# Queries by seven products over pairs of heads, and the experts' stages behind half chunks, in a gated cross-attention layer

## What is computed

```python
def xattn(latents, context, Wq, Wk, Wv, Wo, q_norm_w, k_norm_w):
    kv = concatenate([context, latents], axis=1)              # 461 rows for each of 8 batches
    q = rms_norm(heads(latents @ Wq, 32), q_norm_w)
    k = rms_norm(heads(kv @ Wk, 8), k_norm_w)
    v = heads(kv @ Wv, 8)
    probs = softmax(einsum('bhgqd,bhkd->bhgqk', q, k) / sqrt(128))
    return merge(einsum('bhgqk,bhkd->bhgqd', probs, v)) @ Wo  # 4096 -> 1024
x = x + tanh(g_xattn) * xattn(layernorm(x), context, ...)
x = x + tanh(g_ffn) * experts(layernorm(x))                   # router, top 2 of 8, rank 16
```

## Time and profile before

| | us |
|---|---|
| three runs | 1750.63, 1753.11, 1757.34 |
| median | 1753.11 |
| profiled execution | 1748.85 |
| its span, first to last instruction | 1746.9 |
| granted TensorE clock, mean | 0.995 of full |
| projections end, first query matmul | 636.44 |
| slots 0 to 54 | about 684 to 1309 |
| last chunk ends | about 1701 |

### The profile page before, as it was taken

One profiled execution on the slowest core, in us unless ns is written; L12 is line 12 of the kernel. 1 busy time (PEld: TensorE's weight loads), 2 busy tenths in 40 slices (PEclk: granted clock), 3 DMA queues, 4 the chain that ended last, 5 costly groups with the idle time before them and its releaser, 6 DMA issues.

```text
span 1746.9 us, 26303 instructions
## 1 busy us (share of the span) xinstructions
PE 1692.9 (97%) x9312; PEld 1508.2 (86%) x9312; DVE 1170.6 (67%) x2074; ACT 879.1 (50%) x1655; POOL 730.5 (42%) x584
## 2 busy tenths in 40 slices
PE   7999999999999999999999999999998999999996
PEld 6788888678888879999999999999997888999994
DVE  6778876777777733777777777777766664455546
ACT  5455554454544423666666666666656654343321
POOL 1444543234443402666666666666665550000000
PEclk9999999999999999999999999999999999999999
DMA  5567778545566554344444333444444654665522
GB/s 193 163 185 237 231 213 247 140 145 173 158 176 161 138 214 144 120 122 123 131 130 123 119 122 120 131 131 130 127 126 160 207 181 160 218 218 191 194 102 66
DMA packets 215654, 278.13 MB, mean 159 GB/s; under 512 B 51956, under 2 KB 187956, under 8 KB 210020
## 3 DMA queue, kind: packets, MB, share of 16 engines
q1 hardware_dynamic: 214948, 269.90, 49.7%
q10 hardware_dynamic: 576, 6.55, 0.9%
HBM read 189.77 MB, written 86.64 MB: 158 GB/s over the span
## 4 chain that ended last, share of the span: by engine, by line
PE 87%; DVE 5%; ACT 3%; issue 2%; DMA 2%; POOL 0%; SPq 0%; DVEq 0%; ACTq 0%; POOLq 0%
PE bank L757 26%; PE bank L759 25%; PE bank L758 25%; PE bank L895 5%; PE bank L862 2%; PE bank L791 1%; DVE mx L1652 1%; PE bank L1045 1%; DMA at_raw<-at_d 1%; DMA kT<-kT_d 1%; DVE wo_lo L1672 1%; ACT w_hi L1111 1%; DVE pT_lo L1646 1%; DMA wr<-Wkv 0%; ACT pT_hi L1286 0%
## 5 line engine op out<-in xcount | busy, mean ns | idle before, releaser
L739 POOL TENSOR_SCALAR pr<-pr,rr 100x461 f32<-100x461 f32 x256 | 382.8, 1501 | 299.0 <-DVE rr L1667 299.0
L757 PE MATMUL bank<-w_hi,a_hi 128*128 128x512 f32 (+1 forms) x856 | 340.7, 398 | 12.2 <-DVE a_lo L1442 9.3
L759 PE MATMUL bank<-w_hi,a_lo 128*128 128x512 f32 (+1 forms) x856 | 334.9, 391 | 0.0
L758 PE MATMUL bank<-w_lo,a_hi 128*128 128x512 f32 (+1 forms) x856 | 334.3, 391 | 0.0
L1295 ACT ACTIVATE pr<-bank,nm,rq 100x461 f32<-100x461 f32 x256 | 188.6, 737 | 170.9 <-DVE nm L1658 167.8
L1652 DVE TENSOR_REDUCE mx<-bank 100x1 f32<-100x461 f32 x256 | 161.7, 632 | 81.4 <-PE bank L759 76.1
L757 PEld LDWEIGHTS bank<-w_hi,a_hi 128*128 128x128 f32 (+1 forms) x856 | 157.8, 184 | 49.5 <-issue 10.4
L759 PEld LDWEIGHTS bank<-w_hi,a_lo 128*128 128x128 f32 (+1 forms) x856 | 157.5, 184 | 38.0
L757 PE MATMUL bank<-xT_hi,wq_hi 128*128 128x400 f32 x512 | 188.2, 368 | 0.5 <-issue 0.5
L757 PE MATMUL bank<-at_hi,wo_hi 128*128 128x400 f32 x512 | 183.1, 358 | 5.7 <-DVE at_lo L1683 2.9
L758 PEld LDWEIGHTS bank<-w_lo,a_hi 128*128 128x128 f32 (+1 forms) x856 | 158.0, 185 | 34.8
(11 more groups left out here) (133 smaller groups left out, 3496.1 us busy)
## 6 DMA issues: line engine op xcount, KB each, us to landing
wo_raw<-Wo SPq DMA_DIRECT2D x32, 1024.0 KB, 4.9
kT_d<-kst SPq DMA_DIRECT2D x56, 512.0 KB, 5.2
v_d<-vst SPq DMA_DIRECT2D x56, 512.0 KB
at_raw<-at_d SPq DMA_DIRECT2D x32, 800.0 KB, 7.2
kT<-kT_d SPq DMA_DIRECT2D x64, 361.0 KB, 4.7
kvr<-ctxT SPq DMA_DIRECT2D x44, 512.0 KB, 5.8
wq_raw<-Wq SPq DMA_DIRECT2D x32, 512.0 KB, 6.0
vv<-v_d SPq DMA_DIRECT2D x64, 240.0 KB
```

What stands on the lines that cost most here:

```text
L739: pool.tensor_scalar(pr[0:NQ, u % 2, i], pr[0:NQ, u % 2, i], rr[0:NQ, i:i + 1], None, ALU.mult).then_inc(p_done, 1)
L757: pe.matmul(o, lh, rh, start=start, stop=False, skip_group_check=more)
L758: pe.matmul(o, lh, rl, start=False, stop=False, skip_group_check=more)
L759: return pe.matmul(o, ll, rh, start=False, stop=stop, skip_group_check=more)
```

## The change

**Queries.** The 64 products become 16 steps of two heads by both batch halves, each in seven products of 4 parts (`QSTEPS`, `QORDER`). They continue `SEQ` and the ring of the projections: Wq of two heads goes into `kvr` as a left operand, POOL sums it, ACT and DVE split seven operands a step. The right operands are seven combinations of the latents, made in the second half of the projections (`latents_sum`, `latents_hi`, `latents_lo` on pairs of batches), stored, and loaded as `xw` and `xv`. Results are combined in `cb` and `q_raw`: ACT keeps three of the products, DVE makes four results (`query_result`), and ACT squares them from SBUF. `LEAD` = 16 products run ahead of the first slot (64 parts), the rest in slots 0 to 54, 7 parts a slot. **Experts.** Stages follow half chunks by `FFN_AT`, y is made by ACT with a bias and a scale that POOL makes in two instructions more, and x1 has four buffers. Tiles are laid out anew; the first two pieces of Wo are loaded ahead of slot 54.

```diff
+QSTEPS = H // 2
+QORDER = (P1, P2, P6, P5, P7, P3, P4)
+SEQ += [(_k, _o) for _k in range(STEPS, ALL) for _o in QORDER]
+LEAD = 16
+PRE = PROJ + LEAD
-AHEAD = 9
+OUT0 = -(-(QSTEPS * Q_PARTS - LEAD) * KC // Q_PARTS)
+FFN_AT = {7 * t + a: (t, i) for t in range(B // 2) for i, a in enumerate((0, 2, 3, 5, 6))}
...
@@ SP @@
-            load_chunk_weights(0)
-            load_chunk_weights(1)
+            def load_heads(u):
+                k = QK0 + u // 4 + 1
+                if u % 4 < 2 and k < ALL:
+                    load_kv(k, u % 4)
             for u in range(UNITS):
                 if u == OUT0 - 2:
+                    sp.wait_ge(prod_done, POS[ALL - 1, P6] + 1)
+                    load_chunk_weights(0)
+                    load_chunk_weights(1)
                     load_chunk(0)
                     load_chunk(1)
@@ POOL @@
             for u in range(UNITS):
+                k = QK0 + u // 4
+                if u % 4 == 0 and QK0 < k < ALL:
+                    last_sum(k)
+                if u % 4 == 2 and k + 1 < ALL:
+                    sums(k + 1)
+                if u % 4 == 3 and k + 1 < ALL:
+                    second_sum(k + 1)
                 if u + 1 < UNITS:
                     unit_rms(u + 1)
@@ PE, slot(u) @@
-                n = u + AHEAD if u < LAST_Q else None
+                n = 4 * (QK0 - STEPS + u // 4)
                 def c_(c):
-                    if n is not None:
-                        query_part(n, c)
+                    part = KC * LEAD + Q_PARTS * u + c
+                    if part < KC * Q_PARTS * QSTEPS:
+                        query_part(*SEQ[PROJ + part // KC], part % KC)
...
+                if u % 4 == 3:
+                    squares(n + 2)
...
+                    if u % 4:
+                        squares(n + (0, 1, 3)[u % 4 - 1])
...
-                c_(7)
@@ ACT, slot(u) @@
+                if turn == 0:
+                    operand_of(k, P5)
+                if turn == 1:
+                    operand_of(k, P3)
+                    operand_of(k, P4)
...
                 exps(u, 1)
+                if turn == 0:
+                    query_squares(n)
+                if turn == 1:
+                    keep_p5_q(k)
+                if turn == 2:
+                    query_squares(n + 1)
+                if turn == 3:
+                    query_squares(n + 3)
@@ DVE, slot(u) @@
                 maxima(u, 0)
                 if prev:
                     p_split(u - 1, 0)
-                if n < 2 * H:
-                    copy_queries(n)
+                if turn == 0:
+                    query_result(n)
+                if turn == 1:
+                    operand_of(k, P3)
...
                 inverse(u, 1)
+                if turn == 0:
+                    operand_of(k, P5)
+                if turn == 1:
+                    operand_of(k, P4)
...
                 inverse(u, 3)
+                if turn == 0:
+                    operand_of(k, P7)
+                if turn == 2:
+                    query_result(n + 2)
                 if u + 1 < UNITS:
                     q_split(u + 1)
-                    next_wq(n)
@@ experts @@
+            def norm(t):
+                act.wait_ge(rs2_done, t + 1)
+                if t >= 2:
+                    act.wait_ge(t2_done, t - 1)
+                act.activation(y[0:NQ, t % 2], x1[0:NQ, t % 4], ACT.Identity, bias=mv2[0:NQ, t, 3:4],
+                               scale=mv2[0:NQ, t, 1:2]).then_inc(y_done, 1)
...
+            for n in range(4 * G):
+                for i in range(2):
+                    chunk_head(2 * G + n // 2, n % 2 * 2 + i)
+                if n in FFN_AT:
+                    stages[FFN_AT[n][1]](FFN_AT[n][0])
```

More of the change, by code:

```diff
@@ new lines, in build @@
+        wo_lo = at("wo_lo", LO, [P, 2, R, 512], F32R)
+        at_hi = at("at_hi", AOP, [P, 2, TB, QW], F32R)
+        at_lo = at("at_lo", LO + 16 * KB, [P, 2, TB, QW], F32R)
+        oT = (at("oT0", HI + 32000, [P, C, TW]), at("oT1", LO + 32000, [P, C, TW]))
+        x1 = at("x1", TMP, [P, 4, D])
+        y = at("y", LO + 44800, [P, 2, D])
+        yT = at("yT", HI + 22784, [P, 2, C, NQ])
+        x2 = at("x2", RAW + 8 * KB, [P, 2, D])
+        xr = at("xr", RAW, [P, 2, D])
+        ar = at("ar", WR + 22784, [P, C, AE])
@@ L379, in kv_need @@
         def kv_need(k):
-            return 16 * sum(1 + (n % NT == MIXED) for n in range(k % 2, k + 1, 2))
+            return 16 * sum(1 + (n < STEPS and n % NT == MIXED) for n in range(k + 1) if slot_of(n) == slot_of(k))
         def a_src(i):
             k, o = OPS[i]
-            raw = kvr[:, k % 2]
-            n = cols(k % NT)
+            raw = kvr[:, slot_of(k)]
+            n = rows_of(k)
             if k in PLAIN:
@@ L722, in at_product @@
                     last_sum(k)
-                if o == P5 and k + 1 < STEPS and k + 1 not in PLAIN:
+                if o == P5 and k + 1 not in PLAIN:
                     sums(k + 1)
+                if (k, o) == (STEPS - 1, P4):
+                    second_sum(STEPS)
+                if (k, o) in XSUM_AT:
+                    latents_sum(*XSUM_AT[k, o])
                 if o == P2 and 0 <= k - 1 - X0 < B:
                     latent_rstd(k - 1 - X0)
-            for j in range(PRODUCTS + 3):
+            for j in range(PRE):
                 at_product(j)
@@ L861, in squares @@
                     o = ps[SS][0:NQ, c0:c0 + 2]
-                    mm = pe.matmul(o, sq[:, n % 2, bb * NQ:(bb + 1) * NQ], ones[:], start=True, stop=True)
+                    mm = pe.matmul(o, sq[n % 2][:, bb * NQ:(bb + 1) * NQ], ones[:], start=True, stop=True)
                 mm.then_inc(ss_done, 1)
-            for n in range(AHEAD):
-                for c in range(C):
-                    query_part(n, c)
-                    if n < 2 and c == 4:
-                        turn_keys(STEPS - 1, n)
-                    if n >= 1 and c == 4:
-                        squares(n - 1)
+            for j in range(PROJ):
+                at_product(j)
+            for j in range(PROJ, PRE):
+                k, o = SEQ[j]
+                n = 4 * (k - STEPS)
+                if ("turn0", j) in WHEN:
+                    turn_keys(WHEN["turn0", j], 0)
+                if ("turn1", j) in WHEN:
+                    turn_keys(WHEN["turn1", j], 1)
+                if o == P7:
+                    squares(n)
+                if o in (P1, P2, P6) and k > STEPS:
+                    squares(n - 3 + QORDER.index(o))
+                for c in range(KC):
+                    query_part(k, o, c)
             def scores(u, i):
@@ new lines, in load_x, with keep_query @@
+            def load_x(i, n, m):
+                act.wait_ge(xs_stored, 32 * TB)
+                act.dma_start(xv_hi[:, n - 2:m - 2].bitcast(F32), xh_d[:, n:m]).then_inc(xop_in[i], 16)
+                act.dma_start(xv_lo[:, n - 2:m - 2].bitcast(F32), xl_d[:, n:m]).then_inc(xop_in[i], 16)
+            def keep_query(k, i, o, done):
+                act.wait_ge(prod_done, POS[k, o] + 1)
+                if k == STEPS and o == P1:
+                    act.wait_ge(kn_done, 2 * (k - 1) + 1)
+                elif k == STEPS and o == P6:
+                    act.wait_ge(v_lo_done, 2 * k)
+                elif o == P5:
+                    act.wait_ge(c11_done, winograd_steps(k))
+                else:
+                    act.wait_ge(c22_done if o == P1 else c12_done, winograd_steps(k - 1))
+                act.activation(cb[:, i, 0:TW], ps[query_bank(k, o)][:, 0:TW], ACT.Copy).then_inc(done, 1)
```

709 lines of the change are left out of this document (406 added, 303 removed).

## The result

The changed kernel takes 1801.63 us (median of four runs, 1801.14 to 1804.89) against 1752.71 before: ratio 1.0279 with the 95% interval 1.0256 to 1.0303. That is slower by 49 us, where 8 us less was forecast, and outside the range of 1722 to 1775. Its profiled span is 1799.7 us, 52.8 more than before.

A forecast was written before the change was run, and what follows sets the result against it. PE, busy for 97% of the span, was taken as the bound. The terms -4.5 - 10.2 + 5.7 + 1.5 + 2.5 - 3.6 = -8.6 us, from the median 1753.11, gave 1745 us; the 8-in-10 range was 1722 to 1775.

The forecast's parts named there:

- PE alone: PE's own time in the slots: 43.24 us per four (the four slots of one step) against 45.48 before.
- Ahead of the first slot, -4.5 us: Before the first slot: 8 fewer query parts of 0.56 us, no other engine near its limit; 4.5 us saved.
- Slots, -10 us: Attention slots: 44.74 us per four against 45.48, times 13.75; 10 us gained, bounds 31 gained and 18 lost.
- C: Third slot of each four: Wq lands 1 us in, POOL's sums delay nm and second maximum; 0.6 us wait.
- B: Second slot of each four: PE waits for POOL, about 0.65 us.
- Rival 2: DVE-POOL meetings in the slots last the whole instruction: a_lo 1.3 us and more, 18 us lost; 1773 us; chance 0.17.
- Slot 54, +5.7 us: Ahead of slot 54: two Wo pieces (2.1 MB) join SP's queue before kT; 5.7 us lost, bounds 3 and 9.
- Projections, +1.5 us: Projections' second half: added subtractions raise DVE to about 85%, PE hides most; 1.5 us lost, bounds 0 and 6.
- Experts' loop, +2.5 us: Experts' loop: x1 on DVE and y on ACT ahead of pieces, two tiles each; 2.5 us lost, bounds 0 and 5.
- The end, -3.6 us net: After the last chunk: last result 5.5 us sooner, less 1.9 moved into the loop; 3.6 us gained, bounds 7 and 0.
- The signs: In the slots: prediction wrong if DVE's a_lo are long, or if PE shows no idle time.
- Rival 3: Waits elsewhere: Wq lands 1 to 2 us later (6 us), projections reach upper bound (4 more); 1755 us; chance 0.19.

The follow-up runs named there:

- e11_small: e8_all with DVE's a_lo in the slots and its q_lo cut to 8 columns each; 1729.64 us in one run.
- e9_y: e8_all with ACT making at_hi ahead of y in the odd half chunks of the experts' loop; 1743.17 us.
- e8_all: Changed kernel with later residual load, xv in SP's queue, operands stored in pieces, kT ahead of Wo, reordered transition, POOL's sums held for q_lo; 1745.77 us.
- e5_kT: Changed kernel with later residual, xv in SP's queue, operands in pieces (1771.48 us), plus slot 54's kT issued ahead of Wo and at_raw; 1763.74 us.
- e3_pieces: Changed kernel with the query operands stored one combination at a time instead of 2.8 MB at each pair's end; 1793.82 us.
- e1_res: Changed kernel with SP's next residual load and finished-tile store several half chunks later, behind loads of Wo and at_raw; 1786.9 us.

## Why the prediction was wrong, point by point

- **PE alone (right in kind, a fifth too large).** 448 parts instead of 512 at 0.56 us: fours of 43.24 us were forecast, 2.24 less than before; with DVE's cuts 43.68 were measured, 1.80 less (e11_small). That is 6 us over 13.75 fours.
- **Ahead of the first slot, -4.5 us (wrong).** The step that failed is "with no other engine near its limit there". The engines had room; the buffer `kst` and the transfers had none. PE lost 9.66 us to a store of 22.85 us and ran on at a low clock. That a store from one buffer holds ACT, and ACT holds PE, had no term in the sum. Even in e9_y the stretch is 0.4 us shorter, not 4.5, as PE still waits 6.5 us in four places.
- **Slots, -10 us (wrong: 3.2 us longer over 52 slots where 9.6 less were forecast; PE's share right, the wait mis-sized).** The mis-sized term is q_lo. It was taken as 0.90 us, from a row in which nothing stood behind the scale, and the sums were priced in C, by what they cost nm and the maximum, since Wq was to land 1 us into C. It landed 3.9 us sooner (906.5, where C starts at 909.4), ahead of B's q_lo. Measured: q_lo of 1.62 us at the end of B and 1.42 at the end of C; the fours took 45.2 us, not 44.74. Over 13 fours that is 6 us. Some 6.4 more are three single losses: 3.6 us in the four with the q_lo of 4.16 us (PE waits 2.7 us at 1001.68 and runs at a granted clock of 0.80 until 1010), 1.4 us in one with a q_lo of 2.77 us (at 1239), and 1.4 us in the first, where the granted clock was 0.87 between 716 and 729. Without the ready sum the fours take 44.68 us against the 44.74 of the forecast, but that agreement is partly luck: PE alone wants 0.44 us more than forecast, and the waits cost 1.0 us, not 1.5 (44.68 - 43.68).
- **Rival 2 (the meeting lasts the whole instruction).** It asked for a_lo of 1.3 us and more and fours of 46.5. The a_lo in the slots took 0.67 us on average and the fours 45.2: it did not come about. The Trainium skill, "SBUF — State Buffer", section "Who interferes with whom", has the lock for the whole instruction. In three places the traces are close to that: q_lo with a sum ready (1.62 us; the whole scale and then 0.57 would be 1.27 + 0.57 = 1.84), q_lo at 997.42 (4.16), and POOL's mv held for all of a wo_lo (2.12 beside 2.24, in e8_all). In a fourth it is not: q_lo beside a scale alone takes 0.90.
- **Slot 54, +5.7 us (right).** 5.5 us measured against 5.1 for the stretch, with 6.36 us of idle time on PE against some 7. That it was forecast and yet is so cheap to take away (e5_kT) shows that it was never a price of the change, only of the place in SP's order.
- **Projections, +1.5 us (wrong).** The step that failed is "have one product group more to land; nothing taken". The bytes were counted and their place was not: 2.8 MB of stores at once ahead of a store on which a single buffer depends. That cost 10.3 us (e3_pieces). Of the 4.9 us that e8_all still loses between these key tiles some 2 lie behind the loads of xw, again bytes ahead of the same store; the added work, which is what the +1.5 priced, can have the rest, but no run shows it. From the start to the first query matmul e8_all loses 6.8 us and e9_y 7.7, more than the upper bound of 6.
- **Experts' loop, +2.5 us (wrong, the largest miss).** 4.4 us with the 1.9 that moved in were forecast, 27.0 measured; 20.0 are SP's wait for x1 ahead of Wo's loads (e1_res). The step that failed is the +2.5: the prediction followed y and x1 on DVE, ACT and POOL and never looked at SP, although the change moves x1 within the loop and with it SP's wait. The sentence on y "ahead of a piece in the other two" was right as a mechanism and cost 1.4 us twice (e9_y).
- **The end, -3.6 us net (right).** 5.8 us less from the last chunk to the last result against 5.5.
- **The signs.** Of the two signs named for a wrong prediction neither came: a_lo took 0.67 us, and PE had some 0.9 us of idle time in nearly every four. They looked only at the slots' meetings of DVE and POOL.
- **Rival 3 (waits add up elsewhere)** pointed to the right side with 1755, but its first half, Wq landing 1 to 2 us later, came out the other way: in slot B Wq landed sooner. The sum of the stretches is 15.2 + 6.6 + 3.2 + 5.5 + 1.2 + 27.0 - 5.8 = 52.9 us; this rival named no order in a queue, and that is what the largest parts were.

With the six edits the time is 1745.77 us against the forecast of 1745. That doesn't make the forecast right: it priced the arithmetic of the change and left out four orders in queues. The agreement is luck, too, as its terms don't agree: in e9_y the first query matmul is 7.7 us later (1.5 forecast), the stretch to slot 1 0.4 us shorter (4.5), and the two slots with slot 54 2.9 us shorter, where 5.1 longer were forecast.

## What to carry to other kernels

When a change adds transfers or moves a stage, write out the queue of SP as you do for an engine: which wait stands ahead of which load, and what single buffer depends on a store behind the new bytes. Follow a wait in a trace to its end before naming a culprit, since the engine named (y on ACT) was only the last link of PE, ACT, DMA, SP, DVE. And where DVE meets POOL, look at what POOL has ready behind the instruction it meets, since one semaphore between them gave back 10 us. A median time to landing is no safe term either: 6.0 us was the median, 3.5 us came, and the sum stood ready where it had not been expected.
